# Preparing the feed-forward weights in earlier stages of a transformer layer, through scratch memory

## The chip, the cores and the metric

The kernel runs on the 8 NeuronCores of one Trainium2 chip. All cores run the same program on different rows of the input; nothing is sent between them. The metric is the device time of the slowest core, in microseconds (us).

## What is computed

One pre-norm layer on x of 8192 tokens by 4096: attention with 32 query heads and one shared key/value head of 128, then a gated feed-forward block whose weights are integers with a scale per output row.

```
def _L0_attn_ref(x, wq, wk, wv, wo):
    q = (x @ wq).reshape(B, T, N_HEADS, HEAD_DIM)
    k = x @ wk
    v = x @ wv
    scores = jnp.einsum('bqhd,bkd->bhqk', q, k) * scale
    scores = jnp.where(causal[None, None], scores, -jnp.inf)
    probs = jax.nn.softmax(scores.astype(jnp.float32), axis=-1)
    out = jnp.einsum('bhqk,bkd->bqhd', probs, v).reshape(B, T, C)
    return out @ wo
def _L0_ffn_ref(x, w_gate, s_gate, w_up, s_up, w_down, s_down):
    g = jnp.einsum('th,ih->ti', xt, w_gate.astype(x.dtype)) * s_gate
    u = jnp.einsum('th,ih->ti', xt, w_up.astype(x.dtype)) * s_up
    h = jax.nn.silu(g) * u
    out = jnp.einsum('ti,hi->th', h, w_down.astype(x.dtype)) * s_down
x = x + _L0_attn_ref(_layernorm(x), wq, wk, wv, wo)
x = x + _L0_ffn_ref(_layernorm(x), w_gate, s_gate, w_up, s_up, w_down, s_down)
```

w_gate and w_up are 11008 by 4096 and w_down is 4096 by 11008, all int32.

## The kernel before

Each core owns 8 tiles of 128 tokens (1024 tokens) and computes keys and values for all 64 tiles itself. The program is written as a list of operations, each for one of five engines (SyncE "sy", GpSimd "gp", TensorE "t", VectorE "v", ScalarE "s"), with the operations that it depends on. Every engine runs its own operations strictly in the order in which the code adds them and waits on semaphores where a dependency is on another engine. DMAs are operations too: "sy" and "gp" only issue them, and an engine that waits for the dependency of one DMA issues none behind it. `P.barrier` makes every engine wait for all others. All helpers issue their DMAs through line 240, so in the profile DMA rows are told apart by their tensors. All buffers lie at fixed offsets in one SBUF arena AR.

The stages, with a barrier between them:

- K/V (lines 363 to 371): for each of 64 tiles, SP loads x into one of two buffers `xt`; `ln_sums` (a sum on VectorE, L258, and a square on ScalarE, L260) of tile i is added before `p1a_rest(i - 1)`, which does the statistics and the apply (L271 to L281), 32 transposes (L305) with 4 evictions (L310), and the K and V matmuls (L341, L352). The x load waits for the apply of the tile two before.
- Q (lines 381 to 430): twice 4 tiles are normalised, then 8 blocks of four wq loads (POOL) and 128 matmuls (L417).
- Attention (lines 454 to 654), with its own interleaving of steps. The change adds nothing to it.
- Output projection (lines 662 to 688): 32 blocks, each with one wo load on POOL (two buffers) and 64 matmuls (L675), two evictions (L681), and two writes to attn_sp on SP.
- Second norm (lines 696 to 721): for each of 8 tiles, SP loads attn_sp and xq, TensorE transposes 32 pieces (L704), VectorE adds (L707), SP writes y_sp, then norm and transposes.
- Gate/up (lines 741 to 848): 86 iterations over blocks i of 128 hidden units. An iteration has 12 weight pieces ("units") of 128 by 1024: 4 of w_gate, 4 of w_up, 4 of w_down. For each, POOL loads the int32 piece and casts it to bf16, TensorE makes 8 transposes (L762), VectorE evicts them (L773). For gate and up 16 matmuls of 512 columns follow (L799), issued one unit late through the list `pending`; for down the transposed piece is written by SP to scratch memory wdt_s. At the end of an iteration ScalarE (L818) and VectorE (L824) form h, and SP writes half of it to h_sp.
- Down projection (lines 861 to 937): strips of wdt_s are loaded by SP, 86 matmuls each (L895), then the scale, a transpose back, the addition of y and the write of out.

The lines that set the order of a unit before:

```
ldw = dma("gp", wbf_in[buf], wsrc, deps=[win_rel.get(buf)], ...)
trs.append(add("t", ... e.transpose(...), [ldw, ld_eye16, pb_rel.get(pbp)]))
tev = add("v", ... e.tensor_copy(dst, pb_t[pbp][:, :]), trs + xd, "wtev")
pending.append(mk_mm())
flush()
```

Of the kernel before, what the change touches and what calls it, by code (L numbers as in the profile page):

```python
# [9 lines left out]
BF16 = mybir.dt.bfloat16  # L10
# [7 lines left out]
D = 4096  # L18
NH = 32
DH = 128  # L20
NJ = D // 128
# [97 lines left out]
def build_nc(T=8192, I_FFN=11008):  # L119
# [3 lines left out]
    OWN = NPOS * 128  # L123
    NI = I_FFN // 128
# [3 lines left out]
    HT = OWN // NHALF  # L128
# [22 lines left out]
    d_wdt = nc.dram_tensor("wdt_s", [NJ, 128, NI * 128], BF16).ap()  # L151
    d_hsp = (nc.dram_tensor("h_sp", [NI, 128, OWN - GTP], BF16).ap()
# [5 lines left out]
    ARENA = 204800  # L158

    with ExitStack() as stk:  # L160
# [31 lines left out]
        xt = [fbuf(PA + i * 16384, D) for i in range(2)]  # L192
        xn = [bbuf(PA + 32768 + i * 8192, D) for i in range(2)]
        xnT = [bbuf(PA + 49152 + i * 8192, D) for i in range(2)]
        wq_sb = [bbuf(PA + 16384 + i * 8192, 8 * 512) for i in range(2)]
        xnqT = bbuf(PA + 49152, NJ * HT)
# [15 lines left out]
        wdtcg = [bbuf(F1B + 16384 + b * 2048, 1024) for b in range(2)]  # L212
        h_i = [bbuf(F1B + 20480 + b * ((OWN * 2 + 511) // 512) * 512, OWN)
               for b in range(2)]
        HIE = F1B + 20480 + 2 * ((OWN * 2 + 511) // 512) * 512
# [99 lines left out]

        ld_ones = add("v", lambda e: e.memset(
# [9 lines left out]
        def p1a_rest(i):  # L326
            par = i % 2
            ap9 = ln_fin(par, xt[par], xn[par], p1_sums.pop(i))
            xt_rel[par] = ap9
# [33 lines left out]
        for i in range(NT):  # L363
            par = i % 2
            ld = dma("sy", xt[par], d_x[i * 128:(i + 1) * 128, :],
                     deps=[xt_rel.get(par)], tag=f"x{i}", stream=f"x{par}")
            p1_sums[i] = ln_sums(par, xt[par], xn[par],
                                 [ld, xn_rel.get(par)])
            if i >= 1:
                p1a_rest(i - 1)  # L370
        p1a_rest(NT - 1)

# [8 lines left out]
        for half in range(NHALF):  # L381
# [17 lines left out]
            for mb in range(8):  # L399
# [262 lines left out]
        for m in range(NJ):  # L662
# [4 lines left out]
            for half in range(NHALF):  # L667
# [20 lines left out]
                att_rel[pp] = sd_  # L688

# [6 lines left out]
        for p in range(NPOS):  # L696
# [24 lines left out]
            prev_yn = evs[-1]  # L721

        P.barrier("endP2c")
# [17 lines left out]
        for i_ffn in range(NI):  # L741
# [3 lines left out]
            for mi, dw in enumerate((d_wg, d_wu, d_wd)):  # L745
                for cg in range(4):
                    buf = ub % 4
                    ub += 1
                    if mi < 2:
                        wsrc = dw[i * 128:(i + 1) * 128,  # L750
                                  cg * 1024:(cg + 1) * 1024]
                    else:
                        wsrc = dw.rearrange("(j q) c -> q j c", q=128)[
                            :, cg * 8:(cg + 1) * 8, i * 128:(i + 1) * 128]
                    ldw = dma("gp", wbf_in[buf], wsrc,
                              deps=[win_rel.get(buf)], tag="wld",
                              stream=f"wl{buf}")
                    pbp = buf % 2
                    trs = []
                    for s in range(8):  # L760
                        trs.append(add("t", lambda e, s=s, buf=buf, pbp=pbp:
                                       e.transpose(  # L762
                            pb_t[pbp][:, s * 128:(s + 1) * 128],
                            wbf_in[buf][:, s * 128:(s + 1) * 128], eye16),
                            [ldw, ld_eye16, pb_rel.get(pbp)], "wtr"))
                    win_rel[buf] = trs[-1]
                    if mi < 2:
                        dst = wT[buf]
                        xd = [wT_rel.get(buf)]
                    else:  # L770
                        dst = wdtcg[cg % 2]
                        xd = [wdt_rel.get(cg % 2)]
                    tev = add("v", lambda e, dst=dst, pbp=pbp: e.tensor_copy(  # L773
                        dst, pb_t[pbp][:, :]), trs + xd, "wtev")
                    pb_rel[pbp] = tev

                    if mi == 2:
                        wdst = d_wdt[cg * 8:(cg + 1) * 8, :,
                                     i * 128:(i + 1) * 128].rearrange(
                            "j q c -> q j c")  # L780
                        wd_dma = dma("sy", wdst, wdtcg[cg % 2], deps=[tev],
                                     tag="wdtout", stream=f"wd{cg % 2}")
                        wdt_rel[cg % 2] = wd_dma
                        continue
# [244 lines left out]
```

How the kernel before makes its waits and increments, by code:

```python
        def run_engine(handle, eng):  # L83
# [11 lines left out]
                    if (p["eng"] == eng and e_["fn"] is not None  # L95
                            and e_["sem"] == p["sem"]):
                        pass
                    sname = p["sem"]
                    if satisfied.get(sname, 0) >= p["val"]:
                        continue
                    waits[sname] = max(waits.get(sname, 0), p["val"])
                if eng in CHAIN_ENGS and prev_val is not None:
                    waits[eng] = max(waits.get(eng, 0), prev_val)
                for se, v in sorted(waits.items()):
                    handle.wait_ge(get_sem(se), v)
                    satisfied[se] = v
                if e_["fn"] is not None:
                    inst = e_["fn"](handle)
                    if e_["val"] is not None:
                        inst.then_inc(get_sem(e_["sem"]),
                                      16 if e_["sem"].startswith("D:") else 1)
                elif e_["val"] is not None:
                    handle.nop().then_inc(get_sem(e_["sem"]), 1)
```

## Time and profile before

| | |
|---|---|
| three runs | 12598.06, 12829.56, 12764.45 us (median 12764.45) |
| profiled execution | 12598.06 us, span of the slowest core 12596.5 us |
| spans of the 8 cores | 12476.2 to 12596.5 us, mean TensorE clock 0.823 to 0.833 |
| TensorE matmul busy | 8376.2 us (66%) |
| VectorE, ScalarE, POOL busy | 4372.8, 2887.2, 881.9 us |
| moved by DMA | 932.40 MB, mean 74 GB/s |

PE is TensorE, PEld its weight loads, DVE VectorE, ACT ScalarE, SP SyncE; a q behind a name (SPq, POOLq) is the instruction queue of that engine. The granted clock is given as a share of 2.4 GHz. Busy time of an engine is an average over stages of different kinds, so the stages are to be read one by one. The profile is that of core 4.

### The profile page before, as it was taken

The numbers are of one execution on the slowest core, as the hardware profiler recorded it, in microseconds if no ns is written. First come the engines' busy times: TensorE is split into PE (matmuls) and PEld (weight loads), VectorE is DVE, ScalarE is ACT, GpSimd is POOL, SyncE is SP. The second block draws the span as 40 slices with busy tenths as digits, with TensorE's granted clock in tenths as the row PEclk, the third lists the DMA queues.
The fourth block names the chain that finished last, engine by engine and source line by source line (L and its number), as shares of the span: only waits on it lengthen the run. The fifth ranks groups of instructions, "written<-read, shape, count | busy, mean of one in ns | idle before, by whom it ended". The sixth has DMA issues, their size and how long they took to land.

```text
span 12596.5 us, 152880 instructions; the slowest of 8 cores (12476.2 to 12596.5 us)
## 1 busy us (share of the span) xinstructions
PE 8376.2 (66%) x56100; PEld 4882.8 (39%) x57024; DVE 4372.8 (35%) x7500; ACT 2887.2 (23%) x4272; POOL 881.9 (7%) x1264
## 2 busy tenths in 40 slices
PE   3443765555555555555966888888888886665676
PEld 3333333444444444443433444444444443222222
DVE  4444015666666666666023222222222220000000
ACT  4444003455555555555011000000000000000000
POOL 0000000000000000000101111111111110000000
PEclk7666887777777888888977999899998998777877
DMA  3333661000000000001966777777777773223222
GB/s 121 115 119 113 108 107 34 1 1 1 1 1 1 1 1 1 1 1 14 106 135 124 101 100 105 99 100 105 100 101 105 100 103 109 97 105 130 98 95 96
DMA packets 1144567, 932.40 MB, mean 74 GB/s; under 512 B 878112, under 2 KB 992928, under 8 KB 1132576
## 3 DMA queue, kind: packets, MB, share of 16 engines
q0 software_dynamic: 674880, 412.70, 25.0%
q1 hardware_dynamic: 468960, 509.87, 12.7%
q8 instruction: 474, 7.77, 0.3%
q14 instruction: 253, 2.07, 0.1%
HBM read 1143.94 MB, written 151.78 MB: 103 GB/s over the span
## 4 chain that ended last, share of the span: by engine, by line
PE 50%; DMA 18%; DVE 17%; ACT 8%; issue 7%; DVEq 1%; ACTq 0%; SPq 0%; POOLq 0%; POOL 0%; PEldq 0%
PE ps_a L799 10%; DMA wdt_s<-AR 7%; PE ps_b L799 7%; PE ps_b L895 6%; PE ps_a L895 6%; DVE AR L529 5%; PE pb L568 4%; PE pb L762 3%; PE pf_b L611 3%; DVE AR L258 3%; ACT AR L542 3%; ACT AR L281 2%; DMA AR<-wdt_s 2%; DMA AR<-wq 2%; PE ps_b L500 2%
## 5 line engine op out<-in xcount | busy, mean ns | idle before, releaser
L773 DVE COPY AR<-pb 128x1024 bf16<-128x1024 bf16 x1032 | 697.3, 689 | 2842.6 <-PE pb L762 1987.9
L799 PE MATMUL ps_a<-AR 128*128 128x512 bf16 x5332 | 1354.8, 409 | 9.7 <-DMA AR<-wg 0.2
L500 PE MATMUL ps_b<-AR 128*128 128x512 bf16 x962 | 391.0, 479 | 1283.2 <-ACT AR L542 709.6
L799 PE MATMUL ps_b<-AR 128*128 128x512 bf16 x5331 | 1228.6, 381 | 9.8 <-issue 0.9
L762 PE MATMUL pb<-AR 128*128 128x128 bf16 x8256 | 655.1, 228 | 607.4 <-DVE AR L773 547.7
L568 PEld LDWEIGHTS pb<-AR 128*128 128x128 bf16 x9216 | 778.1, 119 | 615.8 <-issue 547.0
L568 PE MATMUL pb<-AR 128*128 128x128 bf16 x9216 | 931.2, 261 | 82.9 <-ACT AR L594 72.7
L305 PE MATMUL pb<-AR 128*128 128x128 bf16 x2560 | 293.6, 304 | 979.9 <-ACT AR L281 971.6
L818 ACT ACTIVATE AR<-ps_a,AR 128x512 f32<-128x512 f32 x172 | 118.1, 687 | 3521.5 <-PE ps_a L799 3432.8
L895 PE MATMUL ps_a<-AR 128*128 128x512 bf16 x2694 | 699.7, 425 | 322.9 <-DMA AR<-wdt_s 318.1
L895 PE MATMUL ps_b<-AR 128*128 128x512 bf16 x2695 | 701.0, 426 | 283.9 <-DMA AR<-wdt_s 279.5
L762 PEld LDWEIGHTS pb<-AR 128*128 128x128 bf16 x8256 | 549.3, 102 | 827.0 <-issue 681.5
L799 PEld LDWEIGHTS ps_a<-AR 128*128 128x128 bf16 x5504 | 560.9, 105 | 671.7 <-issue 179.1
L799 PEld LDWEIGHTS ps_b<-AR 128*128 128x128 bf16 x5504 | 526.4, 98 | 574.4 <-issue 11.0
L305 PEld LDWEIGHTS pb<-AR 128*128 128x128 bf16 x2560 | 250.6, 138 | 1019.1 <-issue 1013.0
L542 ACT ACTIVATE AR<-ps_a,AR 128x1024 bf16<-128x1024 f32 x576 | 634.8, 1102 | 0.8 <-PE pb L568 0.8
L542 ACT ACTIVATE AR<-ps_b,AR 128x1024 bf16<-128x1024 f32 x576 | 632.1, 1097 | 2.0 <-issue 1.5
L529 DVE TENSOR_REDUCE AR<-ps_b 128x1 f32<-128x1024 f32 x512 | 624.7, 1220 | 21.2 <-PE pb L568 1.7
L500 PE MATMUL ps_a<-AR 128*128 128x512 bf16 x961 | 410.8, 502 | 330.1 <-ACT AR L542 117.2
L536 ACT ACTIVATE AR<-AR 128x1 f32<-128x1 f32 x896 | 265.9, 297 | 1572.9 <-DVE AR L532 1561.3
L260 ACT ACTIVATE AR<-AR 128x4096 bf16<-128x4096 f32 x80 | 289.3, 3617 | 1323.1 <-DMA y_sp<-AR 734.7
L500 PEld LDWEIGHTS ps_b<-AR 128*128 128x128 bf16 x1152 | 77.0, 100 | 1323.2 <-issue 1323.0
(90 smaller groups left out, 10067.3 us busy)
## 6 DMA issues: line engine op xcount, KB each, us to landing
AR<-x SPq DMA_DIRECT2D x64, 2048.0 KB, 7.8
AR<-wdt_s SPq DMA_DIRECT2D x128, 704.0 KB, 8.0
AR<-wg POOLq DMA_DIRECT2D x344, 256.0 KB, 7.2
AR<-wu POOLq DMA_DIRECT2D x344, 256.0 KB, 4.6
AR<-wd POOLq DMA_DIRECT2D x344, 256.0 KB, 4.8
wdt_s<-AR SPq DMA_DIRECT2D x344, 256.0 KB, 5.4
AR<-wdt_s SPq DMA_DIRECT2D x128, 672.0 KB, 7.2
AR<-wq POOLq DMA_DIRECT2D x64, 1024.0 KB, 9.7
```

The costliest lines, as they stand in the source:

```text
L258: e1 = add("v", lambda e: e.reduce_sum(s_sum, src, axis=AX.X), deps_in, "ln_sum")
L260: e2 = add("s", lambda e: e.activation(dst_bf, src, AF.Square, accum_out=s_sq), deps_in + [ln_e5.get(par)], "ln_sq")
L305: e.transpose(p[:, s * 128:(s + 1) * 128], src_bf[:, j * 128:(j + 1) * 128], eye16),
L500: e.matmul(S[:, sh * 512:(sh + 1) * 512], BUF[:, h * OWN + p * 128: h * OWN + (p + 1) * 128], KT[:, n * 1024 + sh * 512: n * 1024 + (sh + ...
L529: rmx = add("v", lambda e, S=S, ph=ph: e.reduce_max(mtmp[ph], S[:, :], axis=AX.X, negate=True), ms_after + [mneg_last.get(ph)], "rmax")
L542: eev = add("s", lambda e, S=S, cp=cp, ph=ph: e.activation(p_sb[cp], S[:, :], AF.Exp, bias=mneg[ph]), ms_after + [bias_ready, p_rel.get(cp ...
L568: trs.append(add("t", lambda e, s=s, cp=cp: e.transpose(pb_t[cp][:, s * 128:(s + 1) * 128], p_sb[cp][:, s * 128:(s + 1) * 128], eye16), [r ...
L611: st_=(s == 0), sp_=(s == 7): e.matmul(o_ps[cp][:, 0:129], pt_sb[cp][:, s * 128:(s + 1) * 128], VSB[:, a * VST: a * VST + 129], start=st_, ...
L762: e.transpose(pb_t[pbp][:, s * 128:(s + 1) * 128], wbf_in[buf][:, s * 128:(s + 1) * 128], eye16),
L773: tev = add("v", lambda e, dst=dst, pbp=pbp: e.tensor_copy(dst, pb_t[pbp][:, :]), trs + xd, "wtev")
L799: e.matmul(psg[mi][hp][:, 0:HT], wT[buf][:, s * 128:(s + 1) * 128], BUF[:, j * OWN + half * HT: j * OWN + (half + 1) * HT], start=(j == 0) ...
L895: mm = add("t", lambda e, i=i, sp=sp, gp_=gp_: e.matmul(psd[gp_], strip[sp][:, i * 128:(i + 1) * 128], h_all[:, i * GTP:(i + 1) * GTP], st ...
```

## The change

All 1032 units (load with cast, 8 transposes, eviction) are taken out of the gate/up stage and put into a function `_emit_prep_unit`, which has three input and three output buffers of its own at the end of the arena and writes every transposed unit to scratch memory with a DMA on SP: the down units to wdt_s as before, the gate and up units to a new tensor wgu_s. `emit_prep(n)` adds the next n units to the program at the place where it is called: 4 after each of the 64 K/V tiles, 3 after each of the 16 Q blocks, 12 after each of the 32 blocks of the output projection, 40 after each of the 8 tiles of the second norm, and the 24 that are left before the gate/up stage. In gate/up each unit becomes one load of 256 KB from wgu_s on SP, ahead of the same 16 matmuls. The K/V stage gets a third `xt` buffer, the arena grows, and some buffers move.

```
+    d_wgu = nc.dram_tensor("wgu_s", [2, NI, 4, 128, 1024], BF16).ap()
-    ARENA = 204800
+    ARENA = 212480
...
-        xt = [fbuf(PA + i * 16384, D) for i in range(2)]
+        xt = [fbuf(PA + i * 16384, D) for i in range(3)]
...
+        pwbf = [bbuf(PWB + b * 2048, 1024) for b in range(3)]
+        pwT = [bbuf(PWB + 6144 + b * 2048, 1024) for b in range(3)]
...
+        def _emit_prep_unit(mi, i, cg):
+            b = pst["ub"] % 3
...
+            ldw = dma("gp", pwbf[b], wsrc, deps=[prep_done.get(("in", b))],
+                      tag="pwld", stream=f"pw{b}")
+            pbp = b % 2
+            trs = []
+            for s in range(8):
+                trs.append(add("t", lambda e, s=s, b=b, pbp=pbp: e.transpose(
+                    pb_t[pbp][:, s * 128:(s + 1) * 128],
+                    pwbf[b][:, s * 128:(s + 1) * 128], eye16),
+                    [ldw, ld_eye16, pb_rel.get(pbp)], "pwtr"))
+            prep_done[("in", b)] = trs[-1]
+            tev = add("v", lambda e, b=b, pbp=pbp: e.tensor_copy(
+                pwT[b], pb_t[pbp][:, :]),
+                trs + [prep_done.get(("T", b))], "pwev")
+            pb_rel[pbp] = tev
+            if mi < 2:
+                od = dma("sy", d_wgu[mi, i, cg], pwT[b], deps=[tev],
+                         tag="pwout", stream=f"pwo{b}")
...
+            prep_done[("T", b)] = od
+            prep_done[(mi, i, cg)] = od
...
         for i in range(NT):
...
             if i >= 1:
                 p1a_rest(i - 1)
+                emit_prep(4)
         p1a_rest(NT - 1)
+        emit_prep(4)
...
                     psq_rel[m] = ev
                     qt_last = ev
+                emit_prep(3)
...
                 att_rel[pp] = sd_
+            emit_prep(12)
...
             prev_yn = evs[-1]
-
+            emit_prep(40)
+
+        emit_prep(10 ** 9)
...
-            for mi, dw in enumerate((d_wg, d_wu, d_wd)):
+            for mi in range(2):
...
+                    tev = dma("sy", wT[buf], d_wgu[mi, i, cg],
+                              deps=[wT_rel.get(buf), prep_done[(mi, i, cg)]],
+                              tag="wTld", stream=f"wt{buf}")
```

Three places show how the order of instructions moves. The first is SP's queue in the K/V stage, before (AR<-x is the load of one tile of x; a NO_OP is a barrier):

```order
L240 DMA AR<-su 128x86
L240 DMA AR<-sd 128x32
L240 DMA AR<-x 128x4096 x64
L113 NO_OP
L240 DMA AR<-xq 128x4096 x8
```

and after (wgu_s and wdt_s are the writes of transposed units):

```order
L244 DMA AR<-x 128x4096 x2
L244 DMA wgu_s<-AR 128x1024 x4
L244 DMA AR<-x 128x4096
L244 DMA wgu_s<-AR 128x1024 x4
L244 DMA AR<-x 128x4096
L244 DMA wdt_s<-AR 128x8x128 x4
```

Every x load but the first two stands behind the four writes of the units that are added after the tile before.

The second is POOL's queue around the output projection, before:

```order
L240 DMA AR<-wq 128x8x512 x64
L113 NO_OP x2
L240 DMA AR<-wo 128x32x128 x32
L113 NO_OP x2
L240 DMA AR<-wg 128x1024 x4
```

and after:

```order
L113 NO_OP x2
L244 DMA AR<-wo 128x32x128
L244 DMA AR<-wu 128x1024 x4
L244 DMA AR<-wd 128x8x128 x4
L244 DMA AR<-wg 128x1024 x4
L244 DMA AR<-wo 128x32x128
L244 DMA AR<-wu 128x1024 x4
```

Between two wo loads there are now twelve loads of units.

The third is SP's queue in the gate/up stage, before:

```order
L240 DMA wdt_s<-AR 128x8x128 x4
L240 DMA h_sp<-AR 128x512
L240 DMA wdt_s<-AR 128x8x128 x4
L240 DMA h_sp<-AR 128x512
L240 DMA wdt_s<-AR 128x8x128 x4
```

and after:

```order
L113 NO_OP
L244 DMA AR<-wgu_s 128x1024 x9
L244 DMA h_sp<-AR 128x512
L244 DMA AR<-wgu_s 128x1024 x8
L244 DMA h_sp<-AR 128x512
L244 DMA AR<-wgu_s 128x1024 x8
```

The four writes per iteration are gone and eight loads have come, of which the first of an iteration stands ahead of the h_sp write of the iteration before and the other seven behind it.

## Rows read from the trace of the kernel before

**Rows 1.** Stretches: busy us (x instructions) of PE, PEld, DVE, ACT, POOL; clock, DMA share, GB/s

```profile
0.00:1200.00 1200.00, 489.63 (x6144) 459.31 (x6144) 538.48 (x770) 500.71 (x257) 5.46 (x8) 0.70 0.33 115
1200.00:1954.00 754.00, 521.47 (x2262) 235.60 (x2304) 103.04 (x144) 62.43 (x32) 54.20 (x62) 0.83 0.65 111
1954.00:5953.00 3999.00, 2283.77 (x20611) 1695.20 (x20994) 2612.81 (x4577) 2140.95 (x3777) 3.35 (x2) 0.80 0.01 2
5953.00:6441.00 488.00, 448.13 (x2007) 200.30 (x2049) 44.28 (x64) 0.00 (x0) 50.27 (x30) 0.98 0.87 107
6441.00:6756.00 315.00, 117.70 (x512) 69.75 (x512) 132.88 (x336) 63.71 (x33) 2.15 (x4) 0.53 0.46 153
6756.00:10438.00 3682.00, 3054.72 (x18919) 1608.26 (x19264) 830.10 (x1290) 119.38 (x173) 668.35 (x1029) 0.92 0.72 102
10438.00:12596.00 2158.00, 1460.78 (x5645) 614.34 (x5760) 111.27 (x320) 0.00 (x0) 98.16 (x129) 0.78 0.29 104
```

**Rows 2.** Chain that ended last, 600 to 637 us (K/V): start us, us, what

```profile
599.64 4.42 DVE AR L258
...
609.54 7.67 DMA AR<-x
617.37 4.42 DVE AR L258
...
636.04 4.41 DVE AR L258
```

**Rows 3.** Timeline, one gate/up iteration: start us, us, instruction, [idle before, releaser]

```profile
8001.36 5.87 PE L799 MATMUL ps_a<-AR 128*128 128x512 bf16 x16
...
8002.41 0.33 SPq L240 DMA_DIRECT2D h_sp<-AR  x1
...
8011.42 3.62 PE L799 MATMUL ps_a<-AR 128*128 128x512 bf16 x16
...
8014.87 0.61 PE L762 MATMUL pb<-AR 128*128 128x128 bf16 x8
...
8037.80 0.69 DVE L773 COPY AR<-pb 128x1024 bf16<-128x1024 bf16 x1 [5.32 <-DMA wdt_s<-AR]
...
8044.35 1.06 PE L799 MATMUL ps_a<-AR 128*128 128x512 bf16 x2
```

**Rows 4.** DMA issues, whole span: tensors, queue, count, KB each, median us to landing

```profile
AR<-wu POOLq DMA_DIRECT2D x344, 256.0 KB, 4.6
...
attn_sp<-AR SPq DMA_DIRECT2D x64, 256.0 KB, 4.0
...
out<-AR POOLq DMA_DIRECT2D x64, 256.0 KB, 2.7
```

**Rows 5.** DMA queue of SP in the K/V stage: packets, MB, share of 16 engines

```profile
q1 hardware_dynamic: 9968, 134.95, 30.7%
```

**Rows 6.** Short stretches of the iteration of rows 3, columns as in rows 1

```profile
8002.00:8004.00 2.00, 2.00 (x6) 0.68 (x5) 1.22 (x3) 0.00 (x0) 0.53 (x1) 0.50 0.30 68
...
8036.00:8044.00 8.00, 1.99 (x18) 1.15 (x16) 1.99 (x4) 0.00 (x0) 0.53 (x1) 0.75 1.16 227
```

**Rows 7.** Chain that ended last, output projection: a load of wo

```profile
6015.53 14.55 DMA AR<-wo
```

**Rows 8.** DMA, output projection: POOL's queue, and loads issued at its end

```profile
q0 software_dynamic: 125931, 32.11, 75.3%
...
AR<-attn_sp SPq DMA_DIRECT2D x1, 2048.0 KB, 10.5
AR<-xq SPq DMA_DIRECT2D x1, 2048.0 KB, 15.3
```

**Rows 9.** Chain that ended last, second norm: writes of y_sp, one per tile

```profile
6501.55 7.66 DMA y_sp<-AR
...
6540.08 7.46 DMA y_sp<-AR
```

**Rows 10.** DMA of the second norm (6441 to 6756): GB/s in 40 slices

```profile
GB/s 177 0 101 266 335 98 2 100 260 345 97 0 133 257 373 37 1 200 240 359 0 2 266 229 304 1 0 301 271 229 0 68 280 305 148 0 146 121 0 55
```

More of the change, by code:

```diff
@@ L191, in build_nc @@
         PA = PH + NT * 256 + ((NT * VST * 2 + 511) // 512) * 512
-        xt = [fbuf(PA + i * 16384, D) for i in range(2)]
[L193 to L196, printed above, removed]
+        xt = [fbuf(PA + i * 16384, D) for i in range(3)]
+        xn = [bbuf(PA + 49152 + i * 8192, D) for i in range(2)]
+        xnT = [bbuf(PA + 65536 + i * 8192, D) for i in range(2)]
+        PWB = ARENA - 12288
+        pwbf = [bbuf(PWB + b * 2048, 1024) for b in range(3)]
+        pwT = [bbuf(PWB + 6144 + b * 2048, 1024) for b in range(3)]
+        wq_sb = [bbuf(PA + 65536 + i * 8192, 8 * 512) for i in range(2)]
+        xnqT = bbuf(PA + 16384, NJ * HT)
         mask_sb = fbuf(PA, NPOS * 1024)
@@ L211, in build_nc @@
         wT = [bbuf(F1B + 8192 + b * 2048, 1024) for b in range(4)]
-        wdtcg = [bbuf(F1B + 16384 + b * 2048, 1024) for b in range(2)]
-        h_i = [bbuf(F1B + 20480 + b * ((OWN * 2 + 511) // 512) * 512, OWN)
+        wdtcg = [bbuf(F1B + 16384 + b * 2048, 1024) for b in range(3)]
+        h_i = [bbuf(F1B + 22528 + b * ((OWN * 2 + 511) // 512) * 512, OWN)
                for b in range(2)]
-        HIE = F1B + 20480 + 2 * ((OWN * 2 + 511) // 512) * 512
+        HIE = F1B + 22528 + 2 * ((OWN * 2 + 511) // 512) * 512
         silu_scr = [fbuf(HIE + b * 2048, 512) for b in range(2)]
@@ L314, in transpose_tile, with emit_prep @@
             return evs
+        prep_units = []
+        prep_done = {}
+        pst = {"ub": 0}
+        def _emit_prep_unit(mi, i, cg):
+            b = pst["ub"] % 3
+            pst["ub"] += 1
+            if mi < 2:
+                wsrc = (d_wg, d_wu)[mi][i * 128:(i + 1) * 128,
+                                        cg * 1024:(cg + 1) * 1024]
+            else:
+                wsrc = d_wd.rearrange("(j q) c -> q j c", q=128)[
+                    :, cg * 8:(cg + 1) * 8, i * 128:(i + 1) * 128]
+            ldw = dma("gp", pwbf[b], wsrc, deps=[prep_done.get(("in", b))],
[12 more added lines that the diff above has]
+            pb_rel[pbp] = tev
+            if mi < 2:
+                od = dma("sy", d_wgu[mi, i, cg], pwT[b], deps=[tev],
+                         tag="pwout", stream=f"pwo{b}")
+            else:
+                wdst = d_wdt[cg * 8:(cg + 1) * 8, :,
+                             i * 128:(i + 1) * 128].rearrange("j q c -> q j c")
+                od = dma("sy", wdst, pwT[b], deps=[tev],
+                         tag="pwdout", stream=f"pwo{b}")
+            prep_done[("T", b)] = od
+            prep_done[(mi, i, cg)] = od
+        for _i in range(NI):
+            for _mi in range(3):
+                for _cg in range(4):
+                    prep_units.append((_mi, _i, _cg))
+        def emit_prep(n):
+            while n > 0 and prep_units:
+                _emit_prep_unit(*prep_units.pop(0))
+                n -= 1
         ld_ones = add("v", lambda e: e.memset(
@@ L327, in p1a_rest @@
             par = i % 2
[L328 to L329 removed]
+            ap9 = ln_fin(par, xt[i % 3], xn[par], p1_sums.pop(i))
+            xt_rel[i % 3] = ap9
             def dst_fn(jg, par=par):
@@ L363, in build_nc @@
         for i in range(NT):
[L364 to L368, printed above, removed]
+            xpar = i % 3
+            ld = dma("sy", xt[xpar], d_x[i * 128:(i + 1) * 128, :],
+                     deps=[xt_rel.get(xpar)], tag=f"x{i}", stream=f"x{xpar}")
+            p1_sums[i] = ln_sums(i % 2, xt[xpar], xn[i % 2],
+                                 [ld, xn_rel.get(i % 2)])
             if i >= 1:
                 p1a_rest(i - 1)
+                emit_prep(4)
         p1a_rest(NT - 1)
+        emit_prep(4)
         P.barrier("endP1a")
```

35 lines of the change are left out of this document (removed).

## Prediction

> **What bounds the kernel now.** I read the stage table first [rows 1], then the chain of waits in the stages that the change touches, then one iteration of the weight stage in the timeline. The seven stretches are: keys and values (K/V), Q, attention, output projection, second norm, gate/up stage, down projection. The reader should see that each is bound by something else. In gate/up TensorE is busy 3055 of 3682 us at a clock of 0.92; in the output projection TensorE (448 of 488) and the DMA engines (share 0.87) are both nearly full; in K/V and in the second norm nothing is full, they are chains.
>
> K/V [rows 2]: a new tile starts every 17.7 us (599.64 to 617.37) or 18.7 us (to 636.04). The chain is sum 4.4, small statistics 1.6, apply 3.8, transposes and K/V matmuls 8 to 9. The 7.67 us load of x ends beside the matmuls, because it is issued at once when the apply is done: SP's queue holds nothing else.
>
> Gate/up [rows 3]: an iteration takes 43.0 us (8001.36 to 8044.35). A group of 16 matmuls takes 3.45 us at the full 2.4 GHz (8011.42 to 8014.87), then 8 transposes. The first group takes 5.87 us [rows 3] at a granted clock of 0.50, the 1.2 GHz level [rows 6], since TensorE had been waiting. It had waited for VectorE, and VectorE for the write of wdt_s (5.32 us of idle before one eviction). So 8 x 3.45 = 27.6 us are matmuls and 15.4 us are transposes, waits and the slow group.
>
> **Part 1: gate/up loses its preparation.** What stays is 86 x 27.6 = 2374 us; at the clock of 0.98 that the output projection holds with matmuls back to back [rows 1] this is 2420. Late next is SP's queue: after each iteration's last matmul the h_sp write waits for the second product (about 1.0 us), takes 0.33 us of SP [rows 3], and the load of the next iteration's second weight group stands behind it (third order fence, eight loads, one write). Its landing is not in this trace: a 256 KB write to out takes 2.7 us and a 256 KB attn_sp write or wu load 4.0 and 4.6 us [rows 4]. So it arrives 1.4 + 2.7 to 4.6 = 4.1 to 6.0 us after the iteration's end, and is needed after 3.45. The stall is 0.6 to 2.5 us per iteration; I take 1.2, near the lower end, since the DMA engines carry little there: 103 us. Gate/up becomes about 2525, a gain of **1150** (1050 to 1240).
>
> **Part 2: what a unit costs in DMA time.** A unit is a 512 KB read of weights (cast to 256 KB), 8 transposes, an eviction and a 256 KB write. In gate/up the engines were busy 0.72 of 3682 us for 1032 units, 2.57 us each [rows 1]. There only a third of the units was written back; now all are, and two thirds are read again. The x loads give a price for contiguous 256 KB: 0.307 x 1200 us for 65 transfers of 2 MB, 0.7 us per 256 KB [rows 5]. So a unit is 2.57 + 0.67 x 0.7 = 3.0 us. Where the engines are full the share reaches 1.16 [rows 6], so back to back I take **2.7 us**. Bounds: 1.4 us, if units moved at the second norm's best rate of 373 GB/s (0.52 MB) [rows 10], and 3.6 us, the rate at which gate/up really went (3682/1032). The value is nearest to the first row because it is the same work.
>
> By the Trainium skill, page "DMA: Bandwidth & Descriptors", section "Anatomy of one DMA — SWDGE (gpsimd) path", a transfer costs 2.0 us plus its bytes at 436 GB/s. That would be an estimate of 3.2 us for one 512 KB read, where the wu row shows 4.6, and 1.8 us per unit back to back, read and write; the sum below would fall by 512 x 0.9, about 460 us, and still be far above before. The trace does not agree with it for these cast loads.
>
> **Part 3: K/V takes 4 units per tile (256).** The third xt buffer allows an earlier x load, but SP's order does not (first fence): each x load now stands behind the four writes of the tile before, the last of which waits for the eviction of the fourth unit. VectorE and ScalarE have the sums of the new tile as next work, ahead of the statistics, evictions and apply of the old one, so the whole chain waits for x. The fourth unit has no free buffer: its load waits for the first one's transposes. One cycle: x 7.8 plus 1.2 for the unit loads beside it, sum 4.6, statistics 1.7, apply 3.9, transposes and K/V matmuls 7.9, transposes of the first unit 0.9, load of the fourth 4.8, its transposes 0.9, eviction 0.8, SP 0.4: **35 us** in place of 18.7. 64 x 35 = 2240 against 1200: **+1040**. Bounds 31 (no contention) and 39.
>
> **Part 4: Q takes 3 units per block of four wq loads (48).** TensorE is not free there: DMA share 0.65 with waits for wq. Each block gets 3 x 3.0 = 9 us of DMA and about 4 us of transposes behind its evictions; some lies in slack. I take 8 us x 16 = **+130** (60 to 200). Attention takes none: 0.
>
> **Part 5: the output projection takes 12 units per block (384).** Before, a block is 15.2 us (488/32) and a wo load lands in 14.55 [rows 7], hidden by two buffers. Now POOL's queue (second fence) has the next wo load behind 12 unit loads, the last of which waits for the ninth unit's transposes. Per block: matmuls 13.8 + 2 for the slow clock after a wait; units 1 to 3 are there, units 4 to 9 at 2.7 each until the twelfth load goes out, about 20 us; then wo, whose own DMA time is 0.753 x 488/30 = 12.2 us [rows 8], behind what is left of loads 10 to 12, about 18 us. **54 us** per block, 1728 in place of 488: **+1240**.
>
> **Part 6: the second norm takes 40 units per tile (320), and 24 units are left.** Before, a tile takes 38.5 us (6501.55 to 6540.08) [rows 9]. Now the attn_sp and xq loads of the next tile stand on SP behind 40 writes, and are exposed: 10.5 and 15.3 us from issue [rows 8]. So 55 us of chain, 2 for the three units already loaded, 37 x 2.7 = 100: 157 us, eight times 1260 in place of 315. With 24 x 2.7 = 65 at the end: **+1010**. The down projection (2158 us) is unchanged.
>
> **Sum.** -1150 + 1040 + 130 + 1240 + 1010 = +2270. The profiled execution took 12598 us (span 12596.5): 14870. It is the fastest of the three shown, whose median is 12764; I say **14,900**.
>
> **Rivals.**
> A, the units slip into idle time. The DMA share is 0.33 in K/V, so 4 units (12 us) do fit in 18 us; if queue order did not matter, K/V and Q cost nothing, and the last two stages are DMA-bound: 728 x 2.7 = 1966 less their idle 0.13 x 488 + 0.54 x 315 = 233, +1733. Sum +583: 13,180. Against it stand the two order fences. 6%.
> B, faster: the same, and the DMA engines stream units at the 373 GB/s of [rows 10], 1.4 us each: 728 x 1.4 - 233 = +786, less 1150: 12,230. It decides from 1.9 us per unit ((1150 + 233)/728) and only with A's overlap. The same loads never came near this pace in gate/up. 3%.
> C, dearer: three buffers and in-order queues let latency add up, units go at 3.6 us (512 exposed ones, +460), K/V at 39 us (+256), wo a few us later (+100): 15,700. For it speaks the 4.6 us of a lone load with only three in flight, against it that gate/up, which gave 3.6, was held by TensorE. 18%.
> D, gate/up gains little, because each stall also brings the 1.2 GHz level for a group as in [rows 3] (2.4 us more, +210): 15,100. 8%, inside the forecast's own range.
>
> **How the numbers follow.** Forecast with D 73%, own range 14,350 to 15,400; A 6%, B 3%, C 18%. The pace's lower bound (1.4 us in Parts 5 and 6 alone, -750) reaches 14,130; I go to 14,200, and to 15,600 above. A measurement here tells about 2% (255 us) from no change: faster 3%, same 2% (a pace between B's and A's), slower 95%.
>
> **What would show it.** Right: an x load issued every 35 us, directly after four writes; ScalarE waiting for x in each tile; blocks of 54 us in the output projection with some 10 us of TensorE waiting for wo; over 150 us per tile in the second norm at a DMA share near 1; gate/up about 2525 us at a clock near 1 with a hole near each h_sp write. Wrong: K/V tiles still near 18 us (A), a second norm tile under 110 us (pace under 1.5), or gate/up above 2800 us.

## Result and profile after

The changed kernel takes 15,700.94 us (median of 12 runs, 15,392.79 to 16,006.54), the kernel before 12,773.79 us (12 runs). In ten of the twelve executions of the changed kernel some of its cores ran at a lower clock and longer than the others, and the ratio of 1.2306, with a 95% interval of 1.22 to 1.2412, compares only executions of both kernels without this: slower by 23%. The forecast was 14,900 us with a range up to 15,600. The direction and the order of the waits came as forecast, the size was too small: +2795 us on the profiled executions (spans 12,596.5 and 15,391.2) where +2270 was expected.

The stages of the changed kernel (core 1), in the order and with the columns of [rows 1]:

```profile
0.00:2527.00 2527.00, 652.48 (x8156) 598.85 (x8157) 709.42 (x1021) 500.73 (x257) 168.82 (x261) 0.61 0.48 107
2527.00:3365.00 838.00, 549.42 (x2727) 259.22 (x2724) 136.59 (x197) 62.43 (x32) 88.23 (x113) 0.84 0.82 132
3365.00:7366.00 4001.00, 2366.43 (x20992) 1687.92 (x20992) 2610.98 (x4576) 2140.91 (x3777) 3.30 (x4) 0.80 0.01 2
7366.00:9395.00 2029.00, 844.39 (x5064) 477.04 (x5064) 298.17 (x440) 0.00 (x0) 297.38 (x407) 0.63 0.82 122
9395.00:10838.00 1443.00, 467.19 (x3320) 338.76 (x3320) 374.47 (x688) 63.72 (x33) 226.68 (x349) 0.51 0.87 163
10838.00:13305.00 2467.00, 2391.37 (x11008) 1071.21 (x11008) 154.44 (x258) 119.38 (x173) 0.76 (x1) 1.00 0.26 78
13305.00:15391.00 2086.00, 1390.74 (x5760) 596.54 (x5760) 110.90 (x320) 0.00 (x0) 98.16 (x129) 0.81 0.30 108
```

The first three numbers to read in each row are its length, the clock (third from the end) and the DMA share (second from the end). Gate/up now runs at clock 1.00 with TensorE busy 97% of the time, so little is left to gain there. What it gave back (1215 us) is lost more than three times over in K/V, the output projection and the second norm (3996 us together), none of which has a clock above 0.63 now. By stage:

| stage | before | after | change | forecast |
|---|---|---|---|---|
| K/V | 1200 | 2527 | +1327 | +1040 |
| Q | 754 | 838 | +84 | +130 |
| attention | 3999 | 4001 | +2 | 0 |
| output projection | 488 | 2029 | +1541 | +1240 |
| second norm, last units | 315 | 1443 | +1128 | +1010 |
| gate/up | 3682 | 2467 | -1215 | -1150 |
| down projection | 2158 | 2086 | -72 | 0 |

The down projection was not changed. Its TensorE busy time went from 1461 to 1391 us, at a clock of 0.78 on core 4 before and 0.81 on core 1 after, and this is nearly all of the 72 us.

One K/V tile in the chain of waits of the changed kernel, which answers to [rows 2] (L338 are the transposes of units, L343 their eviction):

```profile
607.71 0.46 PE pb L338 x8
...
608.71 5.69 DMA AR<-wd
...
614.64 1.02 PE pb L338 x8
...
616.53 0.36 SPq L244
...
617.04 12.82 DMA AR<-x
...
630.02 4.42 DVE AR L262
...
636.04 3.81 ACT AR L285
...
648.66 0.50 PE pb L338 x9
...
649.65 5.50 DMA AR<-wg
...
657.75 11.20 DMA AR<-x
```

The reader should follow it downward. The first unit's transposes end, and only then is the fourth unit's load issued (5.69 us in the chain). Its transposes and eviction follow, then SP issues the write (0.36 us) and behind it x (12.82 us), for which ScalarE and VectorE have been waiting. From x to x it is 40.7 us (617.04 to 657.75) where the kernel before took 17.7 to 18.7. Before, x was issued as soon as the apply was done, and its 7.67 us ran beside the transposes and matmuls of the tile. Now it is issued behind them and behind the units, so that a tile takes all of these times one after the other. Over the stage ScalarE waits for x in each tile, and in the output projection TensorE waits for each wo load (us in total, times, longest):

```profile
ACT AR L264 <- DMA AR<-x: 1844.9, 63, 31.4
...
PE ps_a L730 <- DMA AR<-wo: 483.1, 32, 19.0
```

The second line is 15.1 us per block, where the forecast had some 10.

One block of the output projection, in the same view (compare [rows 7]):

```profile
7979.85 25.04 DMA AR<-wo
...
8005.03 8.91 PE ps_a L730 x32
8013.94 6.91 PE ps_b L730 x32
8020.85 0.50 PE pb L338 x9
...
8022.40 9.13 DMA AR<-wd
...
8033.34 8.08 DMA AR<-wd
...
8046.09 23.64 DMA AR<-wo
```

Matmuls take 15.8 us of 66; then unit loads bind for 25.2 us (8020.85 to 8046.09), then the chain holds nothing but wo for 23.64. The first 32 matmuls take 8.91 us and the next 32 6.91: the granted clock was 0.79 over 8005 to 8014 us and 1.00 over 8014 to 8021, so a group after a wait runs in part at the lower level, as in [rows 3].

In gate/up the hole behind the h_sp write is there, as the timeline shows:

```profile
12012.76 3.62 PE L824 MATMUL ps_a<-AR 128*128 128x512 bf16 x16
...
12013.86 0.32 SPq L244 DMA_DIRECT2D h_sp<-AR  x1
...
12014.33 17.22 SPq L244 DMA_DIRECT2D AR<-wgu_s  x8
...
12017.18 10.52 PE L824 MATMUL ps_a<-AR 128*128 128x512 bf16 x48 [0.80 <-DMA AR<-wgu_s]
```

SP issues h_sp 1.1 us after the group began, the held loads at 1.6 us, and TensorE waits 0.80 us. Over the stage its waits for wgu_s add up to 76.1 us (86 of them), where 103 were forecast.

### The profile page after: what moved, and what is told of

Read it like the earlier page. It is cut to its first block, busy times and chain, and to the rows that moved or that the text cites. A ratio compares the mean times of both kernels' runs of the same rounds, so it can differ in the third digit from the quotient of the medians.

```text
span 15391.2 us, 159185 instructions; the slowest of 8 cores (15297.5 to 15391.2 us)
## 1 busy us (share of the span) xinstructions
PE 8662.0 (56%) x57024; PEld 5029.5 (33%) x57024; DVE 4395.0 (29%) x7500; ACT 2887.2 (19%) x4272; POOL 883.3 (6%) x1264
## 4 chain that ended last, share of the span: by engine, by line
PE 42%; DMA 29%; DVE 14%; issue 7%; ACT 6%; SPq 1%; DVEq 0%; POOL 0%; ACTq 0%; POOLq 0%; PEldq 0%
PE ps_b L824 8%; PE ps_a L824 6%; DMA AR<-wd 6%; DMA AR<-wo 5%; DMA AR<-x 5%; PE ps_b L920 4%; DVE AR L584 4%; PE ps_a L920 4%; PE pb L623 3%; DMA AR<-wu 3%; PE pf_b L666 2%; PE pb L338 2%; DVE AR L262 2%; ACT AR L597 2%; DMA AR<-wg 2%
## 5 line engine op out<-in xcount | busy, mean ns | idle before, releaser
L338 PE MATMUL pb<-AR 128*128 128x128 bf16 x8256 | 884.2, 277 | 1752.4 <-DMA AR<-wd 532.1
L338 PEld LDWEIGHTS pb<-AR 128*128 128x128 bf16 x8256 | 693.5, 124 | 1933.5 <-issue 1921.9
L309 PE MATMUL pb<-AR 128*128 128x128 bf16 x2560 | 293.2, 303 | 1785.7 <-ACT AR L285 1778.3
L824 PE MATMUL ps_a<-AR 128*128 128x512 bf16 x5504 | 1217.3, 379 | 76.1 <-DMA AR<-wgu_s 76.1
L343 DVE COPY AR<-pb 128x1024 bf16<-128x1024 bf16 x1032 | 701.7, 689 | 1917.8 <-PE pb L338 1818.6
L623 PEld LDWEIGHTS pb<-AR 128*128 128x128 bf16 x9216 | 774.2, 119 | 610.0 <-issue 537.3
L623 PE MATMUL pb<-AR 128*128 128x128 bf16 x9216 | 924.0, 259 | 80.6 <-ACT AR L649 70.9
L309 PEld LDWEIGHTS pb<-AR 128*128 128x128 bf16 x2560 | 250.7, 138 | 1830.2 <-issue 1823.7
L920 PE MATMUL ps_a<-AR 128*128 128x512 bf16 x2752 | 661.9, 406 | 321.6 <-DMA AR<-wdt_s 321.6
L849 DVE SCALAR_TENSOR_TENSOR AR<-ps_b,AR 128x512 bf16<-128x512 f32 x172 | 129.1, 751 | 2304.3 <-PE ps_b L824 2304.3
L824 PEld LDWEIGHTS ps_b<-AR 128*128 128x128 bf16 x5504 | 538.6, 98 | 649.3
L555 PE MATMUL ps_a<-AR 128*128 128x512 bf16 x1152 | 466.1, 496 | 294.6 <-ACT AR L597 151.3
L262 DVE TENSOR_REDUCE AR<-AR 128x1 f32<-128x4096 f32 x80 | 353.6, 4420 | 906.6 <-DMA AR<-x 804.6
L649 ACT COPY AR<-pb 128x1024 bf16<-128x1024 bf16 x576 | 577.5, 1003 | 16.9 <-PE pf_b L666 16.9
## 6 DMA issues: line engine op xcount, KB each, us to landing
AR<-x SPq DMA_DIRECT2D x64, 2048.0 KB, 11.6
```

Of the source, the lines that this page charges most:

```text
L262: e1 = add("v", lambda e: e.reduce_sum(s_sum, src, axis=AX.X), deps_in, "ln_sum")
L309: e.transpose(p[:, s * 128:(s + 1) * 128], src_bf[:, j * 128:(j + 1) * 128], eye16),
L338: trs.append(add("t", lambda e, s=s, b=b, pbp=pbp: e.transpose(pb_t[pbp][:, s * 128:(s + 1) * 128], pwbf[b][:, s * 128:(s + 1) * 128], eye16),
L343: tev = add("v", lambda e, b=b, pbp=pbp: e.tensor_copy(pwT[b], pb_t[pbp][:, :]), trs + [prep_done.get(("T", b))], "pwev")
L555: e.matmul(S[:, sh * 512:(sh + 1) * 512], BUF[:, h * OWN + p * 128: h * OWN + (p + 1) * 128], KT[:, n * 1024 + sh * 512: n * 1024 + (sh + ...
L623: trs.append(add("t", lambda e, s=s, cp=cp: e.transpose(pb_t[cp][:, s * 128:(s + 1) * 128], p_sb[cp][:, s * 128:(s + 1) * 128], eye16), [r ...
```

## Experiments

The experiments ran on three chips: all units in one block, x ahead, wo ahead and the first attention run on one; all three orders, the second attention run, four down buffers and the spread on the next; the added wait and the two runs with one barrier on the third. The comparisons rest on the stages of the profiled executions.

**All units in one block.** Edit: `emit_prep(0)` in all four stages, so that the last call, just ahead of gate/up, adds all 1032.

```
-                emit_prep(4)
+                emit_prep(0)
...
-                emit_prep(3)
+                emit_prep(0)
...
-            emit_prep(12)
+            emit_prep(0)
...
-            emit_prep(40)
+            emit_prep(0)
```

> All 1032 units stand in one block before the gate/up stage, none elsewhere. Theory (the units are dear where they stand in the queues between other work, and cost 2.7 us each back to back): the stages before return to the times of the kernel before (1200, 754, 4000, 488, 315 us), the block takes 1032 x 2.7 = 2790, gate/up stays 2467, down projection 2086: about 14,100 us, 8% faster than the changed kernel. Rival (the units cost their DMA time wherever they stand, placement is neutral or the interleaving hides a part): the total stays at 15,400 or rises.

14,486 us (median of 2; profiled 14,538; 14,100 expected). The block of units, and two unit loads from the chain that ended last there:

```profile
6729.00:9676.00 2947.00, 1043.33 (x8256) 798.74 (x8255) 714.35 (x1033) 0.00 (x0) 667.99 (x1029) 0.50 1.11 184
```

```profile
8001.63 6.63 DMA AR<-wu
...
8009.95 6.97 DMA AR<-wd
```

2947/1032 = 2.86 us per unit at a DMA share of 1.11: the forecast's 2.7 was close. What sets this pace is less clear. The chain of the block is load, transposes, next load through the same one of three buffers: 8009.95 - 8001.63 = 8.32 us a round, a third of which is 2.8 us. The landing of a load is part of it, and it is longer here (6.6 us for wu) than in gate/up before (4.6 us [rows 4]) at a DMA share of 0.72. So busier DMA engines and the three buffers may both have a part in it; what more buffers would do was not tested. The stages ahead took their old times (6729 us in all, 6756 before); gate/up took about 2749, since its clock was 0.88 on this core. So hiding the units between other work is dearer than not hiding them at all: gate/up starts at 10,838 us in the changed kernel and at 9676 here, and the profiled runs took 15,391 and 14,536 (spans). The rival of neutral placement falls. But even the plain block costs 2947 us to save 1215.

**x load ahead.** The load of tile i + 1 is issued ahead of the units of tile i (`ld_x` holds the same load as before).

```
...
+        ld_next = ld_x(0)
         for i in range(NT):
             xpar = i % 3
-            ld = dma("sy", xt[xpar], d_x[i * 128:(i + 1) * 128, :], ...)
+            ld = ld_next
+            if i + 1 < NT:
+                ld_next = ld_x(i + 1)
```

> The load of x for tile i+1 is issued ahead of the units of tile i. Theory (SP's queue order exposes the x load): a K/V tile goes from 39.5 us to about 27.3, the stage from 2526 to about 1750, total about 14,610. Rival (the DMA engines are what the stage waits for, the x load only moves its wait to the unit loads): a tile stays above 33 us, the stage above 2100, total above 14,970.

15,039 us (median of 4, from 14,739; profiled 14,739). The ratio to the kernel before is 1.166 (1.148 to 1.184). K/V ends at about 1780 us, 27.8 per tile: near the theory's 1750, and not above 2100. The other stages kept their times but for the down projection, which took 2199 us at a clock of 0.76 on this core (2086 at 0.81 in the changed kernel), so the total fell by 654 us and not by the stage's 747, and missed the 14,610. In the chain a tile now reads

```profile
603.33 6.78 DMA AR<-wd
610.35 1.03 PE pb L338 x8
...
612.08 4.41 DVE AR L262
618.09 3.81 ACT AR L285
622.14 1.87 PE pb L309 x16
```

with no x in it, though x itself still takes 10.3 us to land. The load of the fourth unit (6.78 us) and the two groups of unit transposes are what is left above the old time. The fourth unit waits because there are three input buffers; a fourth buffer was not tried.

**wo load ahead.** The same for the wo load of the next block.

```
...
+        wo_next = ld_wo(0)
         for m in range(NJ):
             wpar = m % 2
-            ldw = dma("gp", wo_sb[wpar], src, deps=[wo_rel.get(wpar)], ...)
+            ldw = wo_next
+            if m + 1 < NJ:
+                wo_next = ld_wo(m + 1)
```

> The wo load of block m+1 is issued on POOL ahead of the 12 unit loads of block m. Theory (POOL's queue order exposes it): TensorE no longer waits for wo, a block goes from 63.3 us to 43 to 48, the output projection from 2029 to 1380 to 1540, total 14,750 to 14,900. Rival (DMA throughput: 0.82 of 63.3 = 52 us of packets per block): a block stays at 55 us or more, the stage at 1760 or more.

15,051 us (median of 2; profiled 15,105), the ratio to the kernel before is 1.188 (1.168 to 1.209).

```profile
7393.00:8983.00 1590.00, 837.27 (x5072) 478.39 (x5072) 302.83 (x441) 0.00 (x0) 296.57 (x407) 0.67 1.03 156
```

TensorE waits for wo once, at the start of the stage, and a block is 1590/32 = 49.7 us: below the rival's 55, a little above the theory's 43 to 48. The DMA share is 1.03: 63.4 x 0.82 = 52 us of packets per block before the edit, 49.7 x 1.03 = 51 after it. The order was the first limit, and the DMA engines, or the three buffers, stand right behind it. The total is above the 14,750 to 14,900 expected: gate/up took 2553 us here, at a clock of 0.96 on this core, where the changed kernel had 2467 at 1.00.

**All three orders mended.** The two edits above, and the attn_sp and xq loads of tile p+1 issued ahead of the 40 units of tile p.

> The changed kernel with all three load orders mended: x ahead of the units in K/V, wo ahead in the output projection, attn_sp and xq ahead in the second norm. Theory (order in the queues is one part, the DMA time of the units the rest): K/V 1780 and output projection 1590 as in the two single runs, second norm with the last units from 1440 to about 1290 (15 to 20 us less per tile), gate/up 2470: total about 14,050, still 11% slower than before. Rival (the parts do not add, since the DMA engines take up what is freed): 14,500 or more.

The profiled run took 14,280 us (14,050 expected), the median of 4 is 14,401; four cores of the profiled run, with a mean clock of 0.78 where the slowest had 0.76, took 13,963 to 13,985. K/V 1770 and output projection 1570 are as alone, and

```profile
8130.00:9424.00 1294.00, 465.96 (x3336) 339.92 (x3336) 373.76 (x689) 63.77 (x33) 227.56 (x350) 0.51 0.96 183
```

for the second norm: 1294 as expected. The stages add up; the 230 us above the expectation lie in gate/up (2566 us at a clock of 0.95) and the down projection (2290 at 0.72) of the slowest core. With its queues in the better order the plan stays some 11% behind the kernel before (13,970 us on those four cores against the 12,580 of its fastest execution on that chip).

**Unit loads behind the large load.** Here the queues keep the order of the changed kernel. Only the dependency list of a unit's load gets one more entry, the x, wo or xq load of its tile or block.

```
-            ldw = dma("gp", pwbf[b], wsrc, deps=[prep_done.get(("in", b))],
+            ldw = dma("gp", pwbf[b], wsrc, deps=[prep_done.get(("in", b)), after],
...
-                emit_prep(4)
+                emit_prep(4, after=ld)
...
-            emit_prep(12)
+            emit_prep(12, after=ldw)
...
-            emit_prep(40)
+            emit_prep(40, after=ldx)
```

> The changed kernel with its queue orders as they are; only the unit loads of a tile or block also wait until the large load of that tile or block (x, wo, xq) has landed. Theory (the large loads land later than forecast, x 11.6 in place of 9 us and wo 23.6 in place of 18, because POOL issues the next three unit loads at once beside or behind them and they share the DMA engines): x lands in 9 us or less, wo in 18 or less; a K/V tile goes from 39.5 to 36 to 37, a block from 63.3 to 57 to 59, total about 15,000 to 15,100. Rival (the unit writes and the loads ahead of them are what delays them): the landings stay within 1 us and the total stays at 15,400 or rises, since three unit loads lose their head start.

14,982 us (median of 2; profiled 14,966). The loads of both kernels, K/V first and then the output projection, as KB each and median us to landing. Changed kernel:

```profile
AR<-x SPq DMA_DIRECT2D x64, 2048.0 KB, 11.6
...
AR<-wo POOLq DMA_DIRECT2D x31, 1024.0 KB, 23.6
```

With the added dependency:

```profile
AR<-x SPq DMA_DIRECT2D x64, 2048.0 KB, 8.5
...
AR<-wo POOLq DMA_DIRECT2D x30, 1024.0 KB, 17.1
```

K/V goes to 2310 us (36.1 per tile), the output projection to 1860 (58.1 per block) and the second norm with the last units to about 1400, where attn_sp and xq land in 9.9 and 14.4 us in place of 15.6 and 20.3. The writes and loads ahead of the large loads were left as they were, so these 3.1, 6.5 and 6 us are not theirs; they may have a part in what is left. The issues behind wo can be seen in the changed kernel, in the block shown above: POOL issues three unit loads before wo has landed at 8004.89.

```profile
7979.85 1.69 POOL L244 DMA_DIRECT2D AR<-wo  x1 [0.39 <-DMA AR<-wg]
7981.53 0.55 POOL L244 DMA_DIRECT2D AR<-wu  x1
7985.12 0.53 POOL L244 DMA_DIRECT2D AR<-wu  x1 [3.04 <-PE pb L338]
7989.51 0.53 POOL L244 DMA_DIRECT2D AR<-wu  x1 [3.87 <-PE pb L338]
```

An added wait made the kernel 425 us faster, by the profiled executions (15,391 and 14,966).

**Units in the attention loop,** where the DMA share is 0.01 [rows 1]. All 1032, one per step, at the end of a step, and `emit_prep(0)` in the other four stages.

```
             if 4 <= it < NR + 4:
                 beatD(recs[it - 4])
+            pst["pbp"] = (it + 1) % 2
+            emit_prep(1)
```

> All units are added to the attention loop, one per step, none elsewhere; attention moves no data by DMA otherwise. Theory A (each unit costs about its eviction of 0.7 us, since VectorE and TensorE have room and the DMA engines are idle): attention goes from 4000 to about 4700 us, the other stages are as in the kernel before, gate/up 2467, total about 12,010, 5% faster than before. Rival B (the units share the two PSUM buffers of the loop, so transposes and eviction, 1.0 + 0.7 us, come into the chain of each step): attention about 5750, total about 13,060, slower than before. Rival C (the queues make TensorE wait for unit loads as elsewhere, 2.7 to 3.5 us a unit): attention 6800 or more, total above 14,000.

13,078 us (median of 4; profiled 13,062), 1.0301 times the kernel before (1.0126 to 1.0476). Attention:

```profile
1905.00:7560.00 5655.00, 3437.08 (x29184) 2397.96 (x29182) 3298.65 (x5599) 2173.43 (x3776) 669.63 (x1032) 0.73 0.62 97
```

5655 - 3999 = 1656 us, 1.6 per unit: rival B's price (1.7). It is the cheapest place of those tried, and still dearer than the 1215 us that gate/up gives back. One wait in this stretch (total us, times, longest) looked like a remedy:

```profile
PE pb L338 <- ACT AR L649: 1588.5, 493, 4.6
```

TensorE waits for ScalarE to release the PSUM buffer that the unit takes over. The plan was to put the unit at the start of a step, into the buffer released in the step before. The edit, against the run just shown:

```
+            pst["pbp"] = it % 2
+            emit_prep(1)
             if it < NR:
                 beatA(recs[it])
...
-            pst["pbp"] = (it + 1) % 2
-            emit_prep(1)
```

> Units in the attention loop again, one per step, but at the start of a step and in the PSUM buffer that was released a step earlier. Theory (in the run with units at a step's end, TensorE waited 1588 us for ScalarE's eviction of the buffer that the unit takes over): about 1.0 us per unit, attention about 5030 in place of 5655, total about 12,400. Rival (it is the work of VectorE and TensorE in a loop that already chains them): attention stays at 5500 or more, total 12,900 or more.

13,142 us (median of 2; profiled 13,001), attention about 5650 us again, and the wait as before (1594.2 us, 493 times). But this run does not test the theory. The end of a step is the place just ahead of the start of the next, and both edits give the unit there the buffer `it % 2`, counted by the step that follows. So the order of operations is the same as in the run before, but for one unit ahead of the first step and one fewer near the end, and the run is a repetition. An earlier place in the step is untested, and whether the shared pair of PSUM buffers or the added work of VectorE and TensorE makes the 1.6 us was not separated.

**Four down buffers in the kernel before.** In the kernel before, VectorE waits in gate/up for the wdt_s writes to release one of two buffers (us in total, times, longest):

```profile
DVE AR L773 <- DMA wdt_s<-AR: 849.3, 168, 11.2
```

The edit gives them four:

```
-        wdtcg = [bbuf(F1B + 16384 + b * 2048, 1024) for b in range(2)]
+        wdtcg = [bbuf(F1B + 16384 + b * 2048, 1024) for b in range(4)]
...
-                        xd = [wdt_rel.get(cg % 2)]
+                        xd = [wdt_rel.get(cg % 4)]
```

> The kernel before with four buffers for transposed down units in place of two (arena 212480); nothing else. Theory (what could be had in gate/up was the wait for the wdt_s writes, not the transposes: 849 us of VectorE idle there): an iteration goes from 42.7 us to 8 x 3.9 + 4 x 0.9 = 35, the stage from 3682 to about 3010, total about 11,930, 5% faster than before. Rival (the DMA engines, 0.72 x 42.7 = 31 us of packets per iteration, or the loads of the four down units in a row take the wait's place): 39 us or more per iteration, total 12,270 or more.

12,422 us (median of 6) against 12,995 (7 runs) of the kernel before on that chip. The two fastest executions of each, 12,328 and 12,351 against 12,580 and 12,594, are only 2% apart. Two cores of the profiled run in the same stretch, core 6 and core 2:

```profile
6800.00:7800.00 1000.00, 924.62 (x6102) 490.87 (x6103) 264.74 (x408) 38.27 (x55) 211.83 (x327) 0.99 0.83 119
```

```profile
6800.00:7800.00 1000.00, 938.56 (x5477) 483.03 (x5575) 241.55 (x375) 34.17 (x50) 193.84 (x299) 0.87 0.76 109
```

6102 matmuls and transposes at 224 per iteration is 27.2 iterations, 36.7 us each; on core 2, whose granted clock stays at 0.87, about 40. The wait for wdt_s is gone on both, and the theory's 35 is nearly met where the clock is 0.99. The pair of cores at 0.87 sets the program's time: they are in the rival's band (39 us or more, total 12,270 or more) for another reason than its own, since their DMA share is only 0.76. The other six ended at 12,033 to 12,261. In four other executions four cores at a mean clock of about 0.85 ended at 11,931 to 12,027 us, where the theory's 11,930 is.

**Down units spread.** The order of the 12 units of an iteration is changed, two buffers kept.

```
-            for mi, dw in enumerate((d_wg, d_wu, d_wd)):
-                for cg in range(4):
+            for mi, cg in ((0, 0), (2, 0), (0, 1), (0, 2), (2, 1), (0, 3),
+                           (1, 0), (2, 2), (1, 1), (1, 2), (2, 3), (1, 3)):
```

> The kernel before, two down buffers, but the four down units stand between gate and up units (every third) and not in a row at the end. Theory (the hole is the run of four writes through two buffers): each write has some 11 us to land, VectorE's wait for wdt_s goes to near 0, an iteration takes about 12 x 0.45 + 27.6 + 1 = 34 us, the stage about 2930, total about 11,850. Rival (DMA-bound): 39 us or more per iteration, total above 12,270.

12,161 us (median of 2; profiled 12,180), against 12,580 for the fastest of the kernel before on that chip; 11,850 was expected, and six of eight cores of the profiled run ended at 11,913 to 11,951. On core 0:

```profile
8500.00:9500.00 1000.00, 983.44 (x6651) 530.50 (x6650) 279.24 (x444) 41.22 (x60) 232.54 (x356) 1.00 0.97 129
```

6651/224 = 29.7 iterations, 33.7 us each, as expected, with TensorE busy 98% and the DMA engines 97%. Without the new scratch tensor this takes most of what the change was to bring to gate/up: 43.0 to 33.7 us per iteration, where the full removal brought 28.7.

**Both, and one barrier.** Four buffers, the spread, and the barrier of line 937 behind the loop over the 64 steps and no longer inside it.

```
-                P.barrier("final")
+        P.barrier("final")
```

> The kernel before with four down buffers, the down units spread between gate and up units, and the barrier at the end of each of the 64 steps of the down projection (line 937, inside the loop) moved behind the loop. Theory for gate/up: 33 to 34 us per iteration on cores at full clock, as with the spread alone, since the DMA share was 0.97 there; stage about 2900 to 3050. Theory for the down projection (each barrier exposes the next strip load): 64 x 86 matmuls x 0.22 = 1211 us plus about 1 us per step, stage about 1280 in place of 2158. Total about 11,050. Rival for the latter (the strips, 2.75 MB per step, are DMA-bound at about 31 us per step beside yld and out): stage stays at 1900 or more, total 11,700 or more.

11,787 us (median of 5; fastest and profiled 11,142) against 12,953 of the kernel before (fastest 12,730). It was run again:

> The kernel of the run before, for an interval against the kernel before: gate/up 2900 to 3050, down projection near 1380, as there; ratio 0.88 to 0.92.

11,529 us (median of 8, from 11,107) against 12,845 (11 runs, from 12,529): 0.898 by the medians, 0.887 by the fastest. There is no interval for it, so the expected band for the ratio is met only by these two figures. Gate/up and down projection of the first of the two profiled runs (11,142 us):

```profile
6834.00:9740.00 2906.00, 2837.94 (x18920) 1538.64 (x19264) 813.51 (x1290) 119.35 (x173) 672.60 (x1028) 1.00 0.96 129
9740.00:11142.00 1402.00, 1243.23 (x5645) 564.38 (x5760) 110.61 (x320) 0.00 (x0) 98.38 (x130) 0.98 0.44 161
```

The down projection goes from 2158 to 1402 us at the same work, and its clock from 0.78 to 0.98. Of the 756 us, 218 are TensorE busy time (1461 to 1243) and the rest is idle time. It stays above the 1280 expected. The rival, that strips are DMA-bound, falls (share 0.44). In the second profiled run (11,355 us) gate/up took 2907 us again, but the down projection 1670, at a clock of 0.80 on the core shown, and not 1380. This version beats both kernels.

## Why the prediction was right and where it was wrong

**Right: gate/up.** 2420 us of matmuls and a stall of 1.2 us per iteration gave 2525, and 2467 came: the matmuls were forecast at a clock of 0.98 and got 1.00 (2391 us busy), the stall behind the h_sp write was 0.9 us (76.1/86), inside the 0.6 to 2.5.

**Right in size: the price of a unit.** Back to back the forecast took 2.7 us, against 2.86 in the run with all units in one block. It was reasoned from DMA time alone; the round through three buffers gives the same price there (8.32/3), and no run separates the two. In the second norm, 143 transposes in 50 us are 17.9 units, 2.8 us each:

```profile
9700.00:9750.00 50.00, 17.93 (x143) 13.62 (x141) 0.50 1.10 188
```

The estimate of 1.8 us per unit, which the prediction worked out from the fit in the Trainium skill, page "DMA: Bandwidth & Descriptors", section "Anatomy of one DMA — SWDGE (gpsimd) path", is not what these cast loads and writes do back to back in either stretch: 2.86 and 2.8 us.

**Right: the two orders.** Taking the x load and the wo load from behind the units removed 747 us of K/V and 439 us of the output projection, each as its own stage time shows. The waits of Parts 3, 5 and 6 were the ones in the chain (xq with 17.6 us in one tile of the second norm), and mending the order of Part 6 took 149 us off the second norm.

**Wrong: the landing of the large loads.** This is the step that failed. Three terms of the sum were too small for one cause. Part 3 had "x 7.8 plus 1.2 for the unit loads beside it", 9.0; it was 11.6. Part 5 had wo "behind what is left of loads 10 to 12, about 18 us"; it was 23.6. Part 6 had "10.5 and 15.3 us from issue"; attn_sp and xq took 15.6 and 20.3 us. Part 3 gave 1.2 us to what runs beside x; Parts 5 and 6 counted what stands ahead of the large load and put what is issued behind it at nothing, without a reason. POOL is free to issue the next tile's or block's first three unit loads as soon as buffers come free, and the large load lands later beside them. The run in which those three wait brought x to 8.5, wo to 17.1, attn_sp to 9.9 and xq to 14.4 us, within about 1 us of the forecast's numbers, and a tile to 36.1 and a block to 58.1 where 35 and 54 had been said. It accounts for 2527 - 2310 = 217 of the missing 287 us in K/V, 2029 - 1860 = 169 of the missing 301 in the output projection and about 43 of the missing 118 in the second norm, and that is what is left after three unit loads have lost their head start.

**Wrong, smaller: the unit phase of a block.** Part 5 had about 20 us to the twelfth load; in the block shown it was 25.2, and on average 63.4 - 15.8 - 23.6 = 24 us. These 4 us and the 5.6 of wo make up the 9.4 by which a block exceeds the 54. In the chain of the block the loads of two down units took 9.13 and 8.08 us. The down units landed in 8.2 us in this stage and the gate units in 6.7 (medians); whether their shape or their place in the queue makes the difference was not tested. In K/V the fourth unit's load took 5.5 to 5.7 us in the chain, 4.8 was said. In the second norm, a pace of 2.8 us in place of 2.7 makes some 30 us of the missing 118 (an estimate, 320 units); with the 43 above, some 45 stay open.

**Rivals.** A and B fall: the total is nowhere near 13,180. C's time (15,700) is the measured median, and in part for its reasons: a K/V tile took 39.5 us where it said 39, and its "wo a few us later" was 5.6 us, 180 us where it had 100. Its largest term, units at 3.6 us, did not occur (2.86), and the K/V tile was long mostly by the landing of x, so that the totals agree is in part luck. D did not occur, the clock of gate/up was 1.00. The forecast started from the fastest execution of the kernel before; the profiled execution of the changed kernel, 15,393 us, lies inside the range, and the median of twelve, 15,701, lies 100 us above it. The range was built from the pace of units and the K/V cycle, and the landing of large loads beside small ones had no bound of its own.

## What to carry to other kernels

Work that is moved "into idle time" is paid for in the queue that it stands in: before moving it, write down for SP's and POOL's queue what now stands ahead of the next stage-critical load, and what is issued right behind it and shares the DMA engines with it. In this kernel it paid to let large loads go out before small ones (747 and 439 us) and to make small prefetches wait for a large load (425 us). And read what the removed instructions were waiting for first: two thirds of this change's gain in gate/up could be had by spreading four writes over the iteration, with nothing moved elsewhere. Last, before running an edit of the order, check that it changes the order: of two runs here the second repeated the first.

## What the runs showed that was not expected

In the profiled run with four down buffers, cores 2 and 3 had a granted clock of 0.86 to 0.87 in gate/up (6800 to 7800 and 8500 to 9500 us) where the other six had 0.97 to 0.99, in the same program and at the same time. This pair decides the time: 12,335 and 12,349 against 12,033 to 12,261 us. The changed kernel, with TensorE busy 97% in gate/up, had 0.99 to 1.00 on all eight cores, the run with all units in one block, whose gate/up is the same code, 0.88 on two, 0.92 on two and 0.97 on four. What decides it is open.

The DMA share (the packets' time over 16 engines) reached 1.11 over 2947 us without a break in the run with one block of units, at 184 GB/s. A share of 1 is thus not the ceiling by this measure, and a share near 1 does not by itself say that the DMA engines set the pace.

Moving one barrier out of a loop of 64 steps was worth 756 us of the kernel before, while no placement of the units that was tried beat that kernel at all.
